# Intermediate results of the node update and of edge packing placed in free PSUM columns

## The reference

```python
all_msgs = jnp.einsum('nh,thd->ntd', h, message_W) + message_b      # 8 edge types
msg = all_msgs[src, edge_type]
messages = segment_sum(msg, dst, num_segments=num_nodes)
gi = messages @ gru_w_ih.T + gru_b_ih
gh = h @ gru_w_hh.T + gru_b_hh
r = sigmoid(i_r + h_r); z = sigmoid(i_z + h_z); n = tanh(i_n + r * h_n)
out = layernorm(x + (1.0 - z) * n + z * h)                           # h is x
```

## Time and profile before

| | |
|---|---|
| median of three timed executions | 2024.81 us |
| profiled execution: its time, its span | 2022.53 us, 2020.8 us |
| POOL busy | 1509.2 us (75%), 1597 instructions |
| PE busy | 1461.7 us (72%) |
| DVE busy | 1107.8 us (55%) |
| ACT busy | 606.0 us (30%) |
| granted TensorE clock | 0.826 on average |

### The profile page before, as it was taken

The page is one execution under the profiler, slowest core; times in us unless marked ns, Lnnn a source line. Parts: engine busy times, 40 slices in busy tenths (PEclk is TensorE's granted clock), DMA queues, the critical chain, the costliest instruction groups (busy, mean ns, idle before and its releaser), DMA issues.

```text
span 2020.8 us, 36225 instructions
## 1 busy us (share of the span) xinstructions
PE 1461.7 (72%) x8006; PEld 1132.0 (56%) x8104; DVE 1107.8 (55%) x3739; ACT 606.0 (30%) x1576; POOL 1509.2 (75%) x1597
## 2 busy tenths in 40 slices
PE   2776767777777777777777777777777777777776
PEld 1655655555555555565555555655655555555555
DVE  7886465555555555545455555555555545554554
ACT  3323423222323223232323222322232323232232
POOL 7777777777777777777777777777777777777773
PEclk9877777878888878878888888788788888888887
DMA  5222222222222222222222222222222222222221
GB/s 123 56 61 63 61 61 62 64 61 62 62 64 60 64 60 65 60 65 60 65 60 64 61 64 63 62 65 60 62 62 64 61 64 61 64 60 65 60 65 38
DMA packets 96794, 127.32 MB, mean 63 GB/s; under 512 B 31070, under 2 KB 70941, under 8 KB 96768
## 3 DMA queue, kind: packets, MB, share of 16 engines
q0 software_dynamic: 50720, 103.98, 19.7%
q1 hardware_dynamic: 45850, 23.03, 4.2%
q10 hardware_dynamic: 198, 0.00, 0.0%
HBM read 120.48 MB, written 6.40 MB: 63 GB/s over the span
## 4 chain that ended last, share of the span: by engine, by line
PE 28%; POOL 25%; issue 19%; DVE 12%; DMA 6%; DVEq 5%; ACT 4%; ACTq 0%; POOLq 0%; SPq 0%
POOL rows L574 25%; PE agg L1375 11%; PE msg L1396 8%; DMA rows<-in_x_dram,idx 6%; DVEq L991 4%; PE gates L1428 3%; PE gates L1433 3%; PE turn L1419 2%; DVE work L1011 1%; ACT sums_room L635 1%; DVE root_a L1048 1%; DVE messages_T L1000 1%; PE gates L1429 1%; DVE rstd L1050 1%; ACT loops L635 1%
## 5 line engine op out<-in xcount | busy, mean ns | idle before, releaser
L574 POOL DMA_INDIRECT rows<-in_x_dram,idx x1398 | 1323.3, 947 | 426.5 <-issue 393.2
L1375 PE MATMUL agg<-onehot,rows 128*128 128x128 f32 x3136 | 602.2, 344 | 102.6 <-DMA rows<-in_x_dram,idx 71.7
L1396 PE MATMUL msg<-sums_room,w_type 128*128 128x320 f32 (+1 forms) x1568 | 488.7, 471 | 169.0 <-issue 165.0
L1375 PEld LDWEIGHTS agg<-onehot,rows 128*128 128x128 f32 x3136 | 496.6, 238 | 171.8 <-issue 160.8
L1396 PEld LDWEIGHTS msg<-sums_room,w_type 128*128 128x128 f32 x1568 | 324.2, 214 | 367.7 <-issue 281.5
L635 ACT ACTIVATE sums_room<-agg 128x512 f32<-128x512 f32 x295 | 176.1, 597 | 541.7 <-PE agg L1375 540.2
L984 DVE TENSOR_TENSOR onehot<-code_T,codes 128x640 f32<-128x640 f32 (+1 forms) x295 | 243.4, 866 | 59.2 <-PE agg L1375 58.4
L1023 DVE TENSOR_TENSOR sums_room<-turn,x_turned 128x512 f32<-128x512 f32 x175 | 121.1, 692 | 203.5 <-PE turn L1419 202.9
L1419 PE MATMUL turn<-loops,spread 16*128 16x128 bf16 x700 | 83.8, 252 | 203.7 <-ACT loops L635 203.7
L635 ACT ACTIVATE counts<-cnt 128x192 f32<-128x192 f32 x99 | 32.7, 330 | 595.1 <-PE cnt L1358 595.0
L574 POOL DMA_INDIRECT rows<-in_x_dram,src_T x170 | 167.7, 987 | 55.0 <-issue 50.9
(11 more groups left out here) (169 smaller groups left out, 1204.8 us busy)
## 6 DMA issues: line engine op xcount, KB each, us to landing
rows<-in_x_dram,idx POOLq DMA_INDIRECT x1398, 2.5
x_next<-in_x_dram SPq DMA_DIRECT2D x97, 64.0 KB
x_tile<-in_x_dram SPq DMA_DIRECT2D x97, 64.0 KB
out_dram<-out_tile SPq DMA_DIRECT2D x97, 64.0 KB
rows<-in_x_dram,src_T POOLq DMA_INDIRECT x170, 2.6
work<-in_dst_dram SPq DMA_DIRECT2D x1, 607.5 KB
work<-in_src_dram SPq DMA_DIRECT2D x1, 607.5 KB
work<-in_edge_type_dram SPq DMA_DIRECT2D x1, 607.5 KB
```

The costliest lines, as they stand in the source:

```text
L574: nc.gpsimd.indirect_dma_start(out=to, out_offset=None, in_=x[:, :], in_offset=bass.IndirectOffsetOnAxis(ap=index, axis=0),).then_inc(done ...
L1375: last = nc.tensor.matmul(agg[c][:, ds(offs[c][k] * TYPES, CODES)], (rows_second if second else rows)[:, start + k, :], onehot[c][:, k, :] ...
L1396: nc.tensor.matmul(msg[:, 0:cols], w_type[:, t, :], sums[:, t, 0:cols], start=t == 0, stop=False, skip_group_check=True)
```

## The change

In `finish_sum` the results d, zd and h go into columns 0 to 383 of the PSUM bank `gates`, except for the last two node tiles. `gates_from_x(j)` therefore waits for `t_y` of the tile before (for the last tile it waits for `t_pre`, as before). In packing, the results of "differ", "first", "wrong", "kinds", "low" and the "moves" masks go into free columns of the PSUM bank `codes`; the chain of steps is run piece by piece, since the room holds one piece. "keep", "word" and "moved" still write SBUF. The number of DVE instructions and of their waits stays as it is.

```diff
+            def room(n):
+                return codes[0:ROWS, CODES:CODES + n]
...
+            for (i, a, b), (_, _, wide) in zip(pieces(ROW_EDGES), pieces(ROW_EDGES + 1)):
+                differ = room(wide - a)
+                nc.vector.tensor_tensor(differ, src_row[:, a:wide], dst_row[:, a:wide], ALU.not_equal).then_inc(packing, 1)
+                nc.vector.scalar_tensor_tensor(out=differ, in0=moves_f[:, a:wide], scalar=-0.5, in1=differ, ...)
+                nc.vector.scalar_tensor_tensor(out=keep_f[:, a:wide], in0=moves_f[:, a + 1:wide + 1], scalar=-0.5, in1=differ, ...)
+                wrong = room(b - a)
+                nc.vector.scalar_tensor_tensor(out=wrong, in0=moves_f[:, a + 1:b + 1], scalar=-1.0, in1=keep_f[:, a:b], ...)
+                nc.vector.tensor_reduce(extremes[0:ROWS, i:i + 1], wrong, AX, ALU.max).then_inc(packing, 1)
...
+            def update_room(j):
+                s = of(j)
+                if isinstance(j, int) and j >= NODE_TILES - 2:
+                    return t_d[s], t_zd[s], t_h[s]
+                return [gates[:, n * HID:(n + 1) * HID] for n in range(3)]
...
-                nc.vector.tensor_tensor(t_d[s][:, :], x_tile[s][:, :], t_n[s][:, :], ALU.subtract).then_inc(d_ready, 1)
+                nc.vector.tensor_tensor(d[:, :], x_tile[s][:, :], t_n[s][:, :], ALU.subtract).then_inc(d_ready, 1)
-                nc.vector.tensor_tensor(t_zd[s][:, :], t_d[s][:, :], rz[s][:, HID:2 * HID], ALU.mult).then_inc(zd_ready, 1)
+                nc.vector.tensor_tensor(zd[:, :], d[:, :], rz[s][:, HID:2 * HID], ALU.mult).then_inc(zd_ready, 1)
-                nc.vector.tensor_tensor(t_h[s][:, :], t_zd[s][:, :], t_n[s][:, :], ALU.add).then_inc(h_ready, 1)
+                nc.vector.tensor_tensor(h[:, :], zd[:, :], t_n[s][:, :], ALU.add).then_inc(h_ready, 1)
-                nc.vector.tensor_tensor(t_y[s][:, :], t_h[s][:, :], x_tile[s][:, :], ALU.add).then_inc(y_ready, 1)
+                nc.vector.tensor_tensor(t_y[s][:, :], h[:, :], x_tile[s][:, :], ALU.add).then_inc(y_ready, 1)
...
+                for i, a, b in pieces(ROW_EDGES):
+                    kinds = room(b - a).bitcast(I32)
+                    nc.vector.scalar_tensor_tensor(out=kinds, in0=moves_f[:, a + 1:b + 1], scalar=float(TYPES), in1=type_row[:, a:b], ...)
+                    nc.vector.scalar_tensor_tensor(out=kinds, in0=kinds, scalar=SRC_BITS, in1=src_row[:, a:b], ...)
+                    nc.vector.scalar_tensor_tensor(out=word_row[:, a:b], in0=dst_row[:, a:b], scalar=SHIFT, in1=kinds, ...)
...
+                for i, a, b in pieces(ROW_EDGES - d):
+                    moves = room(b - a).bitcast(I32)
+                    nc.vector.tensor_scalar(moves, word_row[:, a + d:b + d], 1 << (SHIFT + stage), None, ALU.bitwise_and)
+                    nc.vector.copy_predicated(word_row[:, a:b], moves, word_row[:, a + d:b + d]).then_inc(packing, 1)
...
             def gates_from_x(j):
-                wait_used(pe, pre_ready, j)
+                if isinstance(j, int) and j == NODE_TILES - 1:
+                    pe.wait_ge(pre_ready, j)
+                else:
+                    wait_used(pe, y_ready, j)
```

More of the change, by code:

```diff
@@ L837, in pack, with pieces @@
                     make(i, a, b).then_inc(packing, 1)
+            def pieces(width):
+                return [(i, i * PIECE, width if i == 5 else (i + 1) * PIECE) for i in range(6)]
+            def room(n):
+                return codes[0:ROWS, CODES:CODES + n]
             def pack_slots(name, make):
@@ L879, in _ @@
             dve.wait_ge(src_in, ROW_DMAS * 16)
[L880 to L887, removed]
@@ L1112, in make_words @@
             def make_words():
[L1114 to L1122, removed]
+                for i, a, b in pieces(ROW_EDGES):
+                    base = AT["kinds"] - 6 + 3 * i
+                    kinds = room(b - a).bitcast(I32)
+                    dve.wait_ge(packing, base)
+                    nc.vector.scalar_tensor_tensor(out=kinds, in0=moves_f[:, a + 1:b + 1], scalar=float(TYPES), in1=type_row[:, a:b],
+                                                   op0=ALU.mult, op1=ALU.add).then_inc(packing, 1)
+                    dve.wait_ge(packing, base + 1)
+                    nc.vector.scalar_tensor_tensor(out=kinds, in0=kinds, scalar=SRC_BITS, in1=src_row[:, a:b],
+                                                   op0=ALU.logical_shift_left, op1=ALU.bitwise_or).then_inc(packing, 1)
+                    dve.wait_ge(packing, base + 2)
+                    nc.vector.scalar_tensor_tensor(out=word_row[:, a:b], in0=dst_row[:, a:b], scalar=SHIFT, in1=kinds,
+                                                   op0=ALU.logical_shift_left, op1=ALU.bitwise_or).then_inc(packing, 1)
             def move_words(stage):
@@ L1128, in move_words @@
                     dve.wait_ge(carried, 16)
-                pack(f"moves{stage}", lambda i, a, b: nc.vector.tensor_scalar(
-                    moves_row[:, a:b], word_row[:, a:b], 1 << (SHIFT + stage), None, ALU.bitwise_and))
-                pack(f"moved{stage}", lambda i, a, b: nc.vector.copy_predicated(
-                    word_row[:, a:b], moves_row[:, a + d:b + d], word_row[:, a + d:b + d]), ROW_EDGES - d)
+                for i, a, b in pieces(ROW_EDGES - d):
+                    base = AT[f"moves{stage}"] - 6 + 2 * i
+                    moves = room(b - a).bitcast(I32)
+                    dve.wait_ge(packing, base)
+                    nc.vector.tensor_scalar(moves, word_row[:, a + d:b + d], 1 << (SHIFT + stage), None,
+                                            ALU.bitwise_and).then_inc(packing, 1)
+                    dve.wait_ge(packing, base + 1)
+                    nc.vector.copy_predicated(word_row[:, a:b], moves, word_row[:, a + d:b + d]).then_inc(packing, 1)
             def take_src():
```

17 lines of the change are left out of this document (13 added, 4 removed).

## The result

The changed kernel takes 2015.7 us, median of 8 runs (2014.8 to 2018.2); the kernel before takes 2023.5 us in 8 runs (2019.9 to 2025.1). The ratio is 0.9967, 95% interval 0.9958 to 0.9976: 0.33% faster. The profiled execution took 2015.49 us (span 2013.8) against 2022.53 (2020.8).

What follows compares the result with a forecast made beforehand. POOL's gathers, some held by DVE instructions with two SBUF operands, were taken to set the pace. Savings of 3.7 + 0.5 + 0.9 + 0.4 = 5.5 us from 2023.1 gave 2017.6 us, range 2012.6 to 2024.2.

Steps and rivals of the forecast that it cites:

- What bounds the kernel: From 72.47 us to the last gather POOL sets the pace; a gather takes 0.944 us plus a fixed gap of 0.305.
- "Moves" and "moved", 3.7 us: Packing, rounds 3 to 6: 30 gathers lose their whole excess once neither instruction reads two SBUF operands; 3.7 us saved.
- rival (a): Rounds 3 to 6: the predicated copy still holds POOL up, half of the 3.7 is lost, 2019.4 us; chance 0.13.
- The words, 0.5 us: "Kinds", "low", "word" in round 2: 5 gathers with excess 0.95 us; saving 0 to 0.95, taken as 0.5.
- The node update, 0.9 us: After 300 us: `t_zd`, `t_h`, `t_y` lose their second SBUF operand, saving 0.9 of 1.1 us excess; `t_d` keeps two.
- Rival (c): Node update: `t_d` falls into step with the gathers in each of 95 rounds, 2027.1 to 2033.4 us; chance 0.05.
- The gather at 253.48, 0.4 us: One gather of 2.72 us in an unchanged DVE run; earlier savings may shift it, 0.4 us gain taken.
- DVE's 5.1 us, hidden: Rounds 3 to 6: 42 "moves" lose their fast form, adding 5.1 us on DVE, which has room; no cost in time.
- The longer wait of `gates_from_x`, 0: On PE before the gate matmuls: `t_y` is done 14.5 us before `gates` is next written; cost 0.
- PSUM operands, 0: DVE pieces with other results in PSUM: 30 before the check lie on the path, -0.3 to +0.2 us, taken as 0.
- The tail, unchanged: After the last gather: the last two tiles keep their SBUF results, so the tail is as it was.
- Rival (e): By the skill's inference only the fast "moves" ever blocked POOL: a quarter of 3.7 saved, 2022.2 us; chance 0.03.

Runs made afterwards that it cites:

- packing alone: Changed kernel with the old node update: 2022.2 us against 2025.9 for the kernel before, ratio 0.9984; on two slower chips 1.0020 each.
- `t_n` in PSUM: Changed kernel with the tanh result also in `gates` and `t_zd` back in SBUF: ratios 1.0019 and 1.0042 to the kernel before, both on slower chips.
- the extra sums: Changed kernel plus four DVE sums per round, rounds 12 to 97, second operand in SBUF or PSUM: 2057.8 or 2055.0 us, kernel before 2021.6.

## Why the prediction was right, and where it wasn't

Forecast 2017.6 us, 5.5 less than before, with 0.46 on faster and 0.49 on the same; measured 2015.7, 7.8 less, faster. The main term was right. The total came as near as it did by luck in part: of the 7.0 us between the two traces 3.3 to 3.7 are what the packing surely brings, one term came as nothing, and 3.4 (1.4 at 247 to 270 us, 2.0 in the tail) are chance as far as the traces tell. Step by step:

- **What bounds the kernel:** right on the chips where it takes 2022 us: no gather of the changed kernel after 72.8 us waits longer than the fixed gap. Nothing in one trace could tell that on other chips POOL isn't the bound.
- **"Moves" and "moved", 3.7 us:** right in size. The 30 gathers of the four stretches took 32.01 us; the same 30 take 28.31. A predicated copy with its mask in PSUM holds nothing up, so rival (a) is out. The reason given was incomplete: by the rule of two SBUF reads "moves" could hold nothing, for it had one, yet 0.86 of the 3.69 us were in gathers that began during it. Its result's move to PSUM ended that, and took its fast form with it; the runs don't separate the two.
- **The words, 0.5 us:** 5.67 became 5.37 in the trace after (0.3), 4.73 in packing alone (0.94). In the trace after, the first gathers fell into step with "kinds", as the estimate had it. The size depends on where the first gather falls, as said.
- **The node update, 0.9 us:** this term failed; it brought nothing that the trace shows (excess 1.10 and 1.11 us). I took the excess as that of three sums and assumed that `t_d` would keep its share. In fact 26 gathers began during `t_d` in place of 8, and 21 in place of 2 were held. What `t_h` and `t_y` no longer cost paid for it. Rival (c) named this with its condition, step with `t_d`; it came in 21 gathers, not in each round. Why more gathers meet `t_d` stays open: the sums stand 0.03 us apart and a held gather shifts those behind it, but `t_d` was the first that can hold a gather before the change too, and with no sum that holds one 14 began during it. That the rest is removed with `t_n` in PSUM was shown.
- **The gather at 253.48, 0.4 us:** it gained 1.0 us, and 0.35 of the wait behind it. It lies inside the bounds given (-0.4 to 1.2) but for the wait, and is chance: 2.65 and 2.72 in other traces.
- **DVE's 5.1 us, hidden:** 42 x 0.128 = 5.4 us, hidden here (no longer wait of POOL after 72.8 us) and paid on the chips where PE is the bound, where rounds 3 to 6 are longer by 2.8 to 5.0 us on the same chip. The 1.5 us that I put on a round are under the 1.85 that the extra sums give as an estimate of DVE's cover; the forecast had no number for it.
- **The longer wait of `gates_from_x`, 0:** right. The `gates` matmuls behind it (L1458) had 16.8 us of idle time before them, 17.4 in the kernel before, and none that DVE ended.
- **PSUM operands, 0:** measured +6 to +8 ns for a PSUM destination, some 2 us of DVE over the run, off the path. ("Moves" is the exception, counted above.) The estimate from the Trainium skill's VectorE: DVE Perf Modes, section on the TRN2 errata (65 ns more for a PSUM source) isn't seen: `t_y` takes 291 ns with a PSUM source and took 293 with none.
- **The tail, unchanged:** it was 2.0 us shorter, in PE's work that was open at the last gather. Over four traces it goes with the clock in the 5 us before that gather and not with the change; it is no merit of the forecast.
- **Rival (e)** had the Trainium skill, SBUF — State Buffer, section Who interferes with whom: `tensor_tensor` would not stall descriptor generation, so that only the fast "moves" held gathers. The share that (e) put on "moves", a quarter of 3.7, was right: 0.86 us. The rest wasn't: the 344 extra `tensor_tensor` of 0.565 us lengthened the gathers by 36 us. The same section lets an instruction with two SBUF inputs contend with a GpSimd instruction that reads SBUF, and a gather takes its indices from SBUF; whether a held gather waits with that read or with its descriptors no run here tells.

So of the 5.5 us forecast, the packing's 4.2 came as 4.0 (3.3 were left at 247 us, after small losses in front of round 3 and in rounds 7 and 8), the node update's 0.9 as nothing, and the 0.4 as 1.4 by chance. 3.3 and 1.4, the 0.3 by which the traces part after 270 us, and the tail's 2.0 are the 7.0.

## What to carry to other kernels

Where GpSimd's gathers set the pace, look which DVE instructions run when a gather begins: each one with two SBUF inputs, `copy_predicated` with its mask and data there included, holds it for what is left less 0.13 to 0.15 us, and one operand in PSUM ended that here. The fast form of one SBUF input to an SBUF result held gathers as well. Don't count on removing a part of a back-to-back group: with one of four sums left, its holds cost as much as those of the four had. Check the DVE time that the move adds against the path of the round in which it falls: 5.3 us for 42 masks cost nothing here, 3.3 us in front of the one-hots at 250 us were paid in full, and on a chip with another bound the same change is 0.3% slower.

## What the runs showed that I hadn't expected

The kernel before takes 2022 to 2026 us on some chips and 2755 and 2773 us on two others; the changed one took 2016 on one of the first kind and 2761 on one of the second. The clock granted to TensorE is 0.73 instead of 0.83 of 2.4 GHz on average, gathers and DVE's instructions take the same ns within a few, and the semaphores for which ACT's copies wait come up to 7.9 us (on the second chip 9.8) after the matmul's recorded end, while in the faster traces they come within 0.02 us. Each chip was used in one measurement, so these runs don't tell the chip from the moment. The gathers differ as well: 947 ns at the median in three of the fourteen traces, 944 in the others, two of each kind on one chip. A change is to be judged by its ratio on the same chip, and its sign can differ between chips.
